# Back transformation of an in-kernel eigendecomposition moved into the merges; L1, L2, LSTM and output reordered

## The reference

```python
# L0: 8 Euler steps of a graph ODE
# L1: spectral layer
_, U = jnp.linalg.eigh(L_norm)                  # 512 x 512
agg = jnp.einsum('mn,bnd->bmd', U.T, features)
h = jax.nn.relu(agg @ W1 + b1)
out = jnp.einsum('nm,bmd->bnd', U, h @ W2 + b2)
# L2: agg = A_hat @ features; h = relu(batchnorm(agg @ W1.T + b1)) (256 wide); out = batchnorm(h @ W2.T + b2)
# L3: two graph layers, then for p in 1..4: windows of p nodes go through an LSTM of p steps,
#     whose last hidden state replaces the last node of each window
```

## Time and profile before

| | |
|---|---|
| runs | 4364.65 us (4363.6 to 4366.91) |
| profiled execution | 4359.52 us, its span 4357.7 us |
| TensorE, VectorE busy | 2952.5 us (68%), 2978.4 us (68%) |
| ScalarE, GpSimd busy | 982.9 us (23%), 764.9 us (18%) |
| chain that ended last | VectorE 42%, TensorE 39%, issue 7%, ScalarE 6%, GpSimd 5% |
| TensorE's mean granted clock | 0.818 |

### The profile page before, as it was taken

The page is one execution under the profiler, slowest core; times in us unless marked ns, Lnnn a source line. Parts: engine busy times, 40 slices in busy tenths (PEclk is TensorE's granted clock), DMA queues, the critical chain, the costliest instruction groups (busy, mean ns, idle before and its releaser), DMA issues.

```text
span 4357.7 us, 70705 instructions
## 1 busy us (share of the span) xinstructions
PE 2952.5 (68%) x21286; PEld 1968.4 (45%) x21286; DVE 2978.4 (68%) x18190; ACT 982.9 (23%) x3671; POOL 764.9 (18%) x3343
## 2 busy tenths in 40 slices
PE   2899998888888899999710011010064958699998
PEld 1677777777777765555410000000042623354433
DVE  6677888888888868888878889999822122414323
ACT  0222222322322212222210000000013121336532
POOL 0121222222222222333222221111000000000000
PEclk6789999999989959999855555555587979799998
DMA  2000000000000000000000000000000000000000
GB/s 97 2 2 2 2 2 2 2 2 2 2 2 2 2 1 2 2 2 2 1 0 0 0 0 0 0 0 0 0 0 0 0 19 0 0 0 0 1 0 39
DMA packets 3104, 21.16 MB, mean 5 GB/s; under 512 B 432, under 2 KB 560, under 8 KB 1072
## 3 DMA queue, kind: packets, MB, share of 16 engines
q1 hardware_dynamic: 2736, 16.85, 1.0%
HBM read 12.66 MB, written 4.19 MB: 4 GB/s over the span
## 4 chain that ended last, share of the span: by engine, by line
DVE 42%; PE 39%; issue 7%; ACT 6%; POOL 5%; DMA 0%; DVEq 0%; POOLq 0%; ACTq 0%; SPq 0%
PE ps L1023 6%; DVE H L1895 6%; PE ps L710 4%; DVE jq L1469 3%; PE ps L718 3%; POOL step L1077 3%; PE ps L1030 2%; DVE H L1469 2%; POOL C L1078 2%; ACT sz L1290 2%; DVE PQ L1647 2%; PE ps L566 2%; PE ps L660 2%; PE ps L945 2%; DVE SO L1676 1%
## 5 line engine op out<-in xcount | busy, mean ns | idle before, releaser
L718 PE MATMUL ps<-C 128*32 128x131 f32 (+39 forms) x10200 | 379.4, 279 | 16.6 <-DVE C L1664 15.1
L710 PE MATMUL ps<-eye,same 128*128 128x384 f32 x766 | 365.9, 562 | 0.0
L1077 POOL TENSOR_SCALAR step<-XYEG,PQ 128x8 f32<-128x8 f32 (+3 forms) x510 | 158.6, 311 | 1147.7 <-DVE PQ L1647 1147.7
L1290 ACT ACTIVATE sz<-C,PQ 128x4 f32<-128x4 f32 (+3 forms) x510 | 151.6, 297 | 785.0 <-POOL C L1078 785.0
L1023 PE MATMUL ps<-C,V 128*128 128x512 f32 (+1 forms) x504 | 285.9, 724 | 8.4 <-issue 8.4
L718 PEld LDWEIGHTS ps<-C 128*32 128x32 f32 x10200 | 256.6, 115 | 54.5 <-DVE C L1664 20.6
L1274 ACT ACTIVATE tsc<-tsc 128x1 f32<-128x1 f32 x510 | 103.5, 203 | 726.6 <-DVE tsc L1608 726.6
L1469 DVE CUSTOM_DVE_ANT_0 jq<-SO,ps,C 128x10 f32<-128x10 f32 (+14 forms) x1199 | 220.6, 229 | 64.6 <-PE ps L740 12.1
L727 PEld LDWEIGHTS ps<-dots,C 128*128 128x128 f32 x1020 | 172.7, 201 | 182.1 <-DVE dots L1469 94.2
L740 PE MATMUL ps<-C,XYEG 128*128 128x2 f32 (+1 forms) x958 | 186.4, 270 | 101.3 <-POOL C L1078 98.8
L1895 DVE RECIPROCAL H<-H 128x8 f32<-128x8 f32 (+8 forms) x81 | 242.3, 2992 | 2.8
(11 more groups left out here) (515 smaller groups left out, 7414.6 us busy)
## 6 DMA issues: line engine op xcount, KB each, us to landing
out_x<-X SPq DMA_DIRECT2D x4, 1024.0 KB, 3.9
X<-in_x SPq DMA_DIRECT2D x2, 1280.0 KB, 20.3
X<-in_x SPq DMA_DIRECT2D x1, 1536.0 KB, 16.6
eye<-in_eye SPq DMA_DIRECT2D x1, 1026.0 KB, 9.0
WK<-in_adj SPq DMA_DIRECT2D x1, 1024.0 KB, 5.0
adjT<-in_adjT SPq DMA_DIRECT2D x1, 1024.0 KB, 7.0
WK<-in_below SPq DMA_DIRECT2D x1, 1024.0 KB, 11.0
V<-in_wih SPq DMA_DIRECT2D x1, 1024.0 KB, 4.8
```

Source lines behind the costliest of these rows:

```text
L710: mm(ps[:, 7, 0:n], ident, eye[:, 0, 0:n], start=True, stop=True)
L718: m = mm(ps[q * QUAD:(q + 1) * QUAD, 0, 0:c + n], SI[:, b, 0, 2 * j:2 * j + 1].broadcast_to([P, QUAD]), AS[:, b, q, k * QUAD:P + n], start ...
L1077: step(g_.tensor_scalar(step2[:, k:KB, :], this[:, :, 2:4], PQ[:, r % 2, 1:2], None, ALU.mult))
L1290: fn(sz[:, k:KB].unsqueeze(2), SI[:, k:KB, 0, 2 * j + 1:2 * j + 2], ACT.Copy, scale=PQ[:, r % 2, 2:3])
```

## The change

- **Back transformation.** The Gram matrix and the transposes of V are computed in merge 5, the recursion in merges 6 and 7 with its masks and subtractions on GpSimd instead of VectorE, and the reflections are applied in merge 8, on TensorE and ScalarE, to the product of the first eight merges, transposed. Each piece stands in a pass of the merge, ahead of the pass's own waits on that engine. The product behind merge 8 then gives U at once. Line 862's product stays.
- **L1.** VectorE's statistics start right behind the merges. ScalarE normalises a few batches ahead of need. TensorE reads H in place of a staged copy. The way back is done for four batches in one matmul of 512 columns. The statistics for the next layer norm are taken as X is completed.
- **L2.** As in L1 there is no staging and the batches are normalised ahead. ScalarE copies the first layer's result to SBUF (`hidden2`), and VectorE takes the statistics from there; the second part reads it and does not multiply by W1 again. The second and third part have four PSUM buffers.
- **LSTM.** For p = 3 and 4, GpSimd copies the columns of Ct so that each step's input is contiguous (`SPLIT`), and TensorE's wait for both chains between two values of p gives way to waits for the data that a turn reads. p = 1 and 2 read as before.
- **Output.** TensorE transposes Ct directly, VectorE adds, and SyncE stores two batches at a time.

The core of the diff (TensorE, then GpSimd, ScalarE, VectorE):

```diff
+        GRAM, RECUR, APPLY = LOCAL - 2, LOCAL - 1, LEVELS - 1
...
+            def factors(l):
+                pe.wait_ge(S["gram_sb"], 2 * l + 2)
+                for q in range(KB):
+                    c = slice(q * P, (q + 1) * P)
+                    mm(ps[:, 5, c], masked[:, 1, c], Tr[:, c], start=True, stop=True)
+                    m = mm(ps[:, 6, c], masked[:, 0, c], Tt[:, c], start=True, stop=True)
+                m.then_inc(S["y_ps"], 1)
+                pe.wait_ge(S["y_sb"], l + 1)
+                for q in range(KB):
+                    c = slice(q * P, (q + 1) * P)
+                    mm(ps[:, 5, c], Tt[:, c], WY[:, 0, c], start=True, stop=True)
+                    m = mm(ps[:, 6, c], Tr[:, c], WY[:, 1, c], start=True, stop=True)
+                m.then_inc(S["z2_ps"], 1)
...
+            def reflections():
+                pe.wait_ge(S["qn_sb"], APPLY)
+                across(QT)
+                pe.wait_ge(S["uq_sb"], 1)
+                pe.wait_ge(S["x_upd"], 1)
+                for n, q in enumerate(reversed(range(KB))):
+                    c = slice(q * P, (q + 1) * P)
+                    if n > 0:
+                        pe.wait_ge(S["back_done"], KB * n)
+                    for b in range(KB):
+                        m = mm(ps[:, 4, :], V[:, b, c], U[:, b, :], start=(b == 0), stop=(b == KB - 1))
+                    m.then_inc(S["wy_ps"], 1)
+                    pe.wait_ge(S["wy_sb"], n + 1)
+                    mm(ps[:, 5, :], Tt[:, c], urow[:], start=True, stop=True).then_inc(S["w_ps"], 1)
+                    pe.wait_ge(S["w_sb"], n + 1)
+                    for b in range(KB):
+                        o = ps[:, (6, 7, 4, 5)[b], :]
+                        mm(o, ident, U[:, b, :], start=True, stop=False)
+                        mm(o, VT[:, q, b * P:(b + 1) * P], qrow[:], start=False, stop=True).then_inc(S["back_ps"], 1)
+                pe.wait_ge(S["back_done"], KB * KB)
+                across(U)
...
+            def l1_back(g):
+                pe.wait_ge(S["o_sb"], 4 * g + 4)
+                for nb in range(KB):
+                    n = KB * g + nb
+                    if n > 1:
+                        pe.wait_ge(S["l1_done"], n - 1)
+                    for jb in range(KB):
+                        m = mm(ps[:, 2 + n % 2, :], UT[:, jb, nb * P:(nb + 1) * P], OO[:, :, jb * P:(jb + 1) * P],
+                               start=(jb == 0), stop=(jb == KB - 1))
+                    m.then_inc(S["l1_ps"], 1)
...
+            pe.wait_ge(S["c_y_sb"], 2 * NB)
+            for b in range(NB):
+                pe.wait_ge(S["d_r_sb"], 2 * b + 2)
+                if b > 3:
+                    pe.wait_ge(S["d_o_sb"], 2 * (b - 3))
+                for h in range(2):
+                    m = mm(ps[:, 2 * (b % 4), :], W[("l2W2a", "l2W2b")[h]], RL[:, 2 * (b % 2) + h, :], start=(h == 0), stop=(h == 1))
+                m.then_inc(S["d_o_ps"], 1)
...
+            def factors(l):
+                mask = qrow[:, 0:P]
+                if l > 0:
+                    pool.wait_ge(S["zz_sb"], l)
+                    go(g_.tensor_tensor(Tr, Tr, masked[:, 0, :], ALU.subtract))
+                    m = g_.tensor_tensor(Tt, Tt, masked[:, 1, :], ALU.subtract)
+                    if l == LOCAL:
+                        ch.wait()
+                        m.then_inc(S["x_upd"], 1)
+                        return
+                    go(m)
+                product(mask, same[:, l + 1, :], same[:, l, :], ALU.subtract)
+                mb = mask.unsqueeze(1).broadcast_to([P, KB, P])
+                g_.tensor_tensor(blk(masked[:, 0, :]), blk(upper), mb, ALU.mult).then_inc(S["gram_sb"], 1)
+                g_.tensor_tensor(blk(masked[:, 1, :]), blk(lower), mb, ALU.mult).then_inc(S["gram_sb"], 1)
...
+            turned2, turned3 = LSTM_PLAN[0][0] * NB // 2, LSTM_PLAN[0][0] * NB // 2 + 2 * NB // 4
+            for i in range(4):
                 for s in range(2):
+                    pool.wait_ge(hid_ready[s], turned2 + 2 * (i + 1))
+                    b, n = 4 * i + 2 * s, N // 3
+                    g_.tensor_copy(SPLIT[i][:, s * 6 * n:(s + 1) * 6 * n].rearrange("p (k b w) -> p k b w", k=3, b=2),
+                                   Ct[:, b:b + 2, 0:3 * n].rearrange("p b (w k) -> p k b w", k=3)).then_inc(S["split3"], 1)
+            for i in range(4):
+                for s in range(2):
+                    pool.wait_ge(hid_ready[s], turned3 + 3 * (i + 1))
+                g_.tensor_copy(SPLIT[i].rearrange("p (k b w) -> p k b w", k=4, b=4),
+                               Ct[:, 4 * i:4 * i + 4, :].rearrange("p b (w k) -> p k b w", k=4)).then_inc(S["split4"], 1)
...
+                    if lv >= GRAM:
+                        back_transform(lv, it)
...
+            def back_transform(lv, it):
+                if lv == GRAM:
+                    if it == 1:
+                        act.wait_ge(S["gram_ps"], 1)
+                        fn(upper, ps[:, 4, :], ACT.Copy).then_inc(S["gram_in"], 1)
+                    elif 2 <= it < 2 + KB:
+                        act.wait_ge(S["vtr_ps"], it - 1)
+                        fn(VT[:, it - 2, :], ps[:, 7, :], ACT.Copy).then_inc(S["vtr_sb"], 1)
+                elif lv < APPLY:
+                    i = recursion(lv, it)
+                    l = (i - 1) // 2
+                    if i % 2 == 1 and l < LOCAL:
+                        act.wait_ge(S["y_ps"], l + 1)
+                        fn(WY, ps[:, 5:7, :], ACT.Copy).then_inc(S["y_sb"], 1)
+                    elif i > 0 and l < LOCAL:
+                        act.wait_ge(S["z2_ps"], l + 1)
+                        fn(masked, ps[:, 5:7, :], ACT.Copy).then_inc(S["zz_sb"], 1)
+                else:
+                    if it == 0:
+                        act.wait_ge(S["uq_ps"], 1)
+                        fn(U[:, :, :], ps[:, 4:8, :], ACT.Copy).then_inc(S["uq_sb"], 1)
+                    if 2 <= it < 2 + KB:
+                        for b in range(KB):
+                            act.wait_ge(S["back_ps"], KB * (it - 2) + b + 1)
+                            fn(U[:, b, :], ps[:, (6, 7, 4, 5)[b], :], ACT.Copy).then_inc(S["back_done"], 1)
+                    if 1 <= it < 1 + KB:
+                        act.wait_ge(S["wy_ps"], it)
+                        fn(urow[:], ps[:, 4, :], ACT.Copy).then_inc(S["wy_sb"], 1)
+                        act.wait_ge(S["w_ps"], it)
+                        fn(qrow[:], ps[:, 5, :], ACT.Copy, scale=-1.0).then_inc(S["w_sb"], 1)
+                    if it == NEWTON - 1:
+                        act.wait_ge(S["uq_ps"], 2)
+                        fn(QT[:, :, :], ps[:, 4:8, :], ACT.Copy).then_inc(S["uq_sb"], 1)
...
+            for b in range(0, NB, 2):
+                l1_agg(b)
+                l1_agg(b + 1)
+                if b == 0:
+                    act.wait_ge(S["ut_ps"], 1)
+                    fn(UT[:, :, :], ps[:, 0:4, :], ACT.Copy).then_inc(S["ut_sb"], 1)
+                l1_hidden(b)
+                l1_hidden(b + 1)
+                if b + 5 < NB:
+                    ln_relu(b + 4)
+                    ln_relu(b + 5)
...
+                stats = []
+                for nb in range(KB + 1):
+                    n = KB * g + nb
+                    if nb < KB:
+                        dve.wait_ge(S["l1_ps"], n + 1)
+                        xb = X[:, 4 * g:4 * g + 4, nb, :]
+                        tt(xb, xb, ps[:, 2 + n % 2, :].rearrange("p (b d) -> p b d", b=4), ALU.add).then_inc(S["l1_done"], 1)
+                    if nb > 0:
+                        dve.wait_ge(S["l1_done"], n)
+                        for b in range(4 * g, 4 * g + 4):
+                            m = ch.mark(v.bn_stats(lnst[:, b * KB + nb - 1, :], X[:, b, nb - 1, :]))
+                        stats.append(m)
+                for b in range(4 * g, 4 * g + 4):
+                    ln_aggr(b, stats[-1])
+            ln_factors(2)
```

More of the change, by code:

```diff
@@ L380, in build @@
         drow, erow_s = DO[:, 2, :], DO[:, 3, :]
[L382 removed]
+        HS, HS2, AG, HR = (WK[:, 2 * k:2 * k + 2, :] for k in (0, 3, 0, 1))
+        OO = WK[:, 4:8, :]
         RL = WK[:, 2:6, :]
@@ L832, in merge, with gram @@
                     bias_sums(lv)
+                elif lv == GRAM:
+                    gram()
+                elif lv in (RECUR, RECUR + 1):
+                    for l in range(4 * (lv - RECUR), min(4 * (lv - RECUR) + 4, LOCAL)):
+                        factors(l)
+                elif lv == APPLY:
+                    reflections()
+            def gram():
+                for q in range(KB):
+                    for b in range(KB):
+                        m = mm(ps[:, 4, q * P:(q + 1) * P], V[:, b, q * P:(q + 1) * P], V[:, b, q * P:(q + 1) * P],
+                               start=(b == 0), stop=(b == KB - 1))
+                m.then_inc(S["gram_ps"], 1)
+                for q in range(KB):
+                    if q > 0:
+                        pe.wait_ge(S["vtr_sb"], q)
+                    for b in range(KB):
```

(57 more changed lines are left out.)

370 lines of the change are left out of this document (139 added, 231 removed).

## The result

| | before | after |
|---|---|---|
| median of the runs, us | 4364.1 (4 executions, 4358.5 to 4366.9) | 3952.5 (4 executions: 3942.4, 3943.8, 3961.2, 3964.6) |
| profiled execution, us | 4359.5, span 4357.7 | 3942.4, span 3940.4 |
| ratio after to before | | 0.9059, 95% interval 0.9026 to 0.9093 |

A forecast was written before the change was run, and what follows sets the result against it. No engine is busy throughout, so the span was priced as a row of stages; savings less 9.4 us for the merges sum to 402.3, taking 4359.5 to 3957.2, forecast as median 3962, own range 3940 to 3985, with B 3932 to 4006.

The forecast's parts named there:

- Merges: Nine merges: GpSimd operations that outlast the reciprocal spill onto VectorE's products, costing 9.4 us; bounds 0 and 35.
- The collision: Merges: GpSimd and VectorE shut each other out when both work on two SBUF operands; work beside a reciprocal is free.
- the first step has no subtractions and fits: Merge 6: the first recursion step hides beside the 3.35 us reciprocal; three later steps cost 2.1 us each.
- in merge 7 ... all fits: Merge 7: the reciprocal is twice as long as merge 6's, so GpSimd's recursion work there costs nothing.
- LSTM: LSTM stage: unstepped input matmuls in skips 3 and 4 and no barriers between skips, 302.1 against 396.8, 94.7 us saved.
- a chain has half a period of slack, so I count 0: LSTM: 12 new GpSimd copies cost 0; without that slack VectorE's products wait for whole copies, at worst 50 us.
- rival C: LSTM: the step isn't what slows input matmuls, or copies take the gain back; 85 us lost, 4047; chance 0.07.
- Output: Output stage: VectorE's 16 additions bind at 11.5 us, then 3.8 for the last store; 15.3 against 31.2, 15.9 saved.
- L1's start: Last merge to L1: 25.3 us in place of 204.6, 179.3 saved; ScalarE's queue, not TensorE, is late next.
- B: Merges: GpSimd's work is not hidden; all serial it costs 35 us in place of 9.4, 3988; chance 0.13.
- D: Merges to L1: the recursion chain outlasts the passes meant to hide it, some 120 us come back, 4082; chance 0.03.
- E: Merge 8: ScalarE waits for TensorE ahead of VectorE's root, making the kernel slower than before, 4460; chance 0.02.

The follow-up runs named there:

- run 1: Changed kernel with GpSimd's recursion operations of merges 5 to 7 narrowed to 4 columns: 3942.0 us in one execution, the nine merges 982.0 against 995.0.
- run 4: Changed kernel with each of GpSimd's four 2048-element copies for skip 4 cut into four: median 3941.7 us, ratio 0.9059, LSTM 302.6.
- run 3: Changed kernel with TensorE's stepped input reads of skips 3 and 4 restored, GpSimd's copies kept: 4048.5 us in one execution, LSTM 387.5.
- run 2: Changed kernel with the recursion's 14 subtractions moved from GpSimd to TensorE: 3953.7 us in one execution, merges 987.7.

## Why the prediction was right, and where it was off

- **The frame.** The stages behind the merges follow one another, so that each could be read and priced by itself: every term but two came within 2.1 us, and the sum within 6.5 of 402.3. L1, both big parts of L2 and skips 1, 2 and 4 rest in the main on one row: an instruction with 512 columns costs 0.43.
- **Merges, -13.1 for -9.4.** The collision was right (run 1), and its price where I charged it: 1.94 per later step of merge 6 (2.1 forecast), about 1 per part in merge 5. The step that failed is "the first step has no subtractions and fits", and with it "in merge 7 ... all fits". Both are first passes of a merge, in which GpSimd's own chores run longer: in merge 7 the recursion began 4.0 us after the reciprocal's start and cost 2.27; in merge 6 it began 3.1 us after it, and the first step cost 1.94. (The later steps of merge 7 did fit.) I had the chores' end (0.73 after the start) from a later pass.
- **LSTM, 86.7 for 94.7.** "a chain has half a period of slack, so I count 0" failed. In skip 3 the slack is enough for a copy of 1.57 us and not for 3.87; in skip 4, with longer matmuls, it was enough for 3.88. I had written down the condition in the same sentence, and a worst case of 50. The price is three gaps of some 2.2 us and their restarts: run 4 takes back 7.3 in skip 3 and 7.5 in the LSTM; the 0.5 that is left of the 8.0 lies in the first round of skip 3, which is as long in run 4. The step's price (rival C, 85) was right to the microsecond in run 3: 28.9 + 56.5 against the sum's terms.
- **Output, 18.0 for 15.9.** The additions of VectorE stood back to back, 9.48 for 16 in place of 16 x 0.72 = 11.5: each lasts 0.69, but one begins 0.60 after the other. What follows the last of them took 3.7, as charged (3.8).
- **L1's start.** 24.3 for 25.3, and what is late is what was named: the queue of ScalarE.
- **Rivals.** B's mechanism is at work, at 13.1 of its 35. C is out by run 3. D and E left no sign: merge 8's passes stayed 26.5, and the product that gives the transformed vectors began 5.7 us behind the last merge, as it did before.
- **The median.** 3952.5 is 9.5 below the forecast though the change saved 6.5 less than forecast; that it lies so near is in part luck. The rest is the reduction: its clock stayed at half from reflection 336 to 351 in the profile of before and not in two of the four executions after (by their times and mean clocks, 3942 and 3944 at 0.844 and 0.843 against 0.836 and 0.835; of these four only the first was profiled). With the long stretch on both sides the change is worth 396 us, which puts the profiled execution at 3964, and seven of the ten executions lie within 10 us of that. I took the untouched 2160 us for constant; in the nine profiles without added filling they ended between 2140.2 and 2176.6.

The Trainium skill (SBUF — State Buffer, Who interferes with whom) states that VectorE with two SBUF inputs and a GpSimd operation that reads SBUF exclude each other for the whole instruction. The traces agree: 4.21 us for 0.51 beside a copy of 3.87, and 1.45 beside pieces of a quarter (run 4).

## What to carry to other kernels

Where VectorE has slack, price work on GpSimd by its longest single operation against the slack of VectorE's next two-operand product, and cut it until it fits; the total mattered far less (run 4). Where VectorE has none, as in the merges, count every operation that falls past the cover (runs 1 and 2). Read the cover of each added operation in the very pass in which it will stand, as first passes carry extra chores. Before a gain is put down to a change, compare the stages that it did not touch: here 21 of 417 us were a clock that happened to come back.
